# Weighted sums over key blocks 0 and 3, then 1 and 2, with the first half waiting for two causal masks

## The chip, the core and the metric

The kernel runs on one core of a Trainium2 chip. A core has a matrix engine (TensorE, PE in the profile, with its weight loads as PEld), a vector engine (VectorE, DVE), a scalar engine (ScalarE, ACT), a general engine (GpSimd, POOL) and a queue engine that only issues transfers (SyncE, SP). Each works through its own list of instructions in order; semaphores hold one back until another has got far enough. The metric is the device time of one execution in microseconds (us), lower is better.

## The reference, cut to what matters

The program computes one transformer layer on 16 sequences of 512 tokens and 128 features: a layer norm, causal attention with 16 heads of 32 features that share 4 key and value heads (rotary positions, low-rank projections), and beside it a gated feed-forward part whose operands are rounded to blocks of FP4. The part that is changed is this one:

```python
scores = jnp.einsum('bqhd,bkhd->bhqk', q, k) * scale
scores = jnp.where(causal[None, None], -jnp.inf, scores)
w = jax.nn.softmax(scores, axis=-1)
out = jnp.einsum('bhqk,bkhd->bqhd', w, v)
```

## The kernel before

**Stages.** The 16 sequences (batches) go through a software pipeline. One iteration t of the main loop does the row maxima of the scores of batch t+1, the exponentials and most weighted sums of batch t, what is left of batch t-1, and the first projections of batch t+2. It runs for t from -2 to 16; iterations 1 to 14 have all stages, and each takes some 50 us.

**Slots.** Within an iteration TensorE has 8 slots, one for each pair of heads. A slot has six tiles of scores for the row maxima (`max_tile`, L977 and L978, into three PSUM buffers that VectorE reduces in L621), between them five tiles of scores for the exponentials (`exp_tile`, L992, into two PSUM buffers that ScalarE turns into P in L815 and L818), some other jobs from the table MISC (the feed-forward matmuls L1029, transposes, projections, the output job L1076 and L1078), and at the slot's end one half of the weighted sums of a group. A tile is issued only once the buffer's reader is done with the tile two or three before it.

**Groups and the causal mask.** Four heads make a group g. P of a group holds, for each head, four key blocks of 128 keys. Key block kb is multiplied only with the queries that can see it, from kb*128 on, so the blocks 0, 1, 2 and 3 have 512, 384, 256 and 128 columns. The triangle on the diagonal of each block is set to zero by GpSimd: `causal` issues four `affine_select` (L470), one for each block and for all four heads, and each adds 1 to the semaphore `causal_done`. GpSimd does this between its other work (the products of the feed-forward part L477 to L502, the statistics of the layer norm L514 to L519, rotary positions L552 to L566), in the fixed order of its list.

**Weighted sums.** `weighted_sums` (L1011) multiplies V with P into the PSUM tile pv_ps, 32 partitions for each head: two halves for each group. The first half of group 3 of the batch before stands at the end of slot 0 and its second half at the end of slot 1; group 0 has slots 2 and 3, group 1 slots 4 and 5, group 2 slots 6 and 7. Before, the first half does the blocks 0 and 1 (896 columns a head) and the second 2 and 3 (384 columns a head), and the first half waits for all four masks of its group.

**What follows the slots.** Early in slot 1 ScalarE normalizes the next input (`normalize_x`, L885) before that slot's first exponential; it needs `shift` of GpSimd (L519), which stands behind the masks of group 3 in GpSimd's list. Those masks stand behind the addition of L480, which needs VectorE's L609 of slot 7. After that, in slot 1, VectorE reduces xn (L691) and computes scales (L596 to L600) between the maxima of L621.

Of the kernel before, what the change touches and what calls it, by code (L numbers as in the profile page):

```python
# [15 lines left out]
H, KVH = 16, 4  # L16
# [6 lines left out]
NT = S // 128  # L23
# [41 lines left out]
]  # L65

H_POWERS = [(6, 2), (6, 3), (6, 4), (7, 0)]
FIRST_T, LAST_T = -2, B


# [53 lines left out]
def build(nc, x, wqaT, wkvaT, wqb, wkvb, wout, bout, wgate, wup, wdown, cosq, sinq, cosk, sink,  # L124
          mask_q, mask_k, out):
    ctx = ExitStack()
    with ctx:
# [3 lines left out]
        def sem(name):  # L131
            return ctx.enter_context(nc.semaphore(name))
# [131 lines left out]
        causal_done = sem("causal_done")  # L264
# [179 lines left out]
        def _(pool):  # L444
# [19 lines left out]
            def causal(T, off, g):  # L464

                T.wait(pool, exp_done, NPAIR * NEXP, off, 2 * NEXP * (g + 1))
                p = P[g % 2]
                for kb in range(NT):
                    diag = p[:, :, P_COL[kb]:P_COL[kb] + 128]
                    nc.gpsimd.affine_select(out=diag, in_=diag, compare_op=ALU.is_ge, fill=0.0, base=0,  # L470
                                            pattern=[[0, GH], [1, 128]], channel_multiplier=-1).then_inc(causal_done, 1)
# [33 lines left out]
            def iteration(T):  # L505
# [4 lines left out]
                if T.has(-1):  # L510
                    causal(T, -1, 3)
# [27 lines left out]
                if T.has(0):  # L539
                    causal(T, 0, 0)  # L540
# [27 lines left out]
                if T.has(0):  # L568
                    causal(T, 0, 1)
# [231 lines left out]
        def _(act):  # L801
# [86 lines left out]
            def extra(T, slot, r):  # L888
# [23 lines left out]
                if (slot, r) == (2, 1) and T.has(2):  # L912
# [3 lines left out]
                    nc.scalar.activation(x_mag[:, :], xq[:, :], ACT.Copy, scale=2.0 ** 22).then_inc(x_powers, 1)  # L916
                if (slot, r) in H_POWERS and T.has(1):
                    f = H_POWERS.index((slot, r))
                    if f == 0:
# [21 lines left out]
        def _(pe):  # L941
# [3 lines left out]
                             start=True, stop=True).then_inc(factors_joined, 1)  # L945
# [50 lines left out]
            def weighted_sums(T, off, g, second):  # L996

                if not T.has(off):
                    return
                if not second:  # L1000
                    T.wait(pe, exp_done, NPAIR * NEXP, off, 2 * NEXP * (g + 1))
                    T.wait(pe, causal_done, NT * KVH, off, NT * (g + 1))

                    if g % 2 == 0:
                        T.wait(pe, oT_done, 2, off, g // 2)
                    if g == 0:
                        T.wait(pe, v_ready, 2, off, 2)
                for kb in ((2, 3) if second else (0, 1)):
                    width = S - kb * 128
                    for j in range(GH):  # L1010
                        last = nc.tensor.matmul(pv_ps[32 * j:32 * j + 32, kb * 128:S], V[T.par(off)][:, kb, g, :],  # L1011
                                                P[g % 2][:, j, P_COL[kb]:P_COL[kb] + width],
                                                start=(kb == 0 and g % 2 == 0), stop=(kb == NT - 1 and g % 2 == 1))
                if second:
                    last.then_inc(pv_done, 1)

# [64 lines left out]
            def iteration(T):  # L1081
                for slot in range(NPAIR):
                    max_tile(T, slot, 0)
                    exp_tile(T, slot, 0)
                    max_tile(T, slot, 1)
                    exp_tile(T, slot, 1)
                    for job in MISC[slot][0]:
                        misc_job(T, *job)
                    max_tile(T, slot, 2)
                    exp_tile(T, slot, 2)  # L1090
                    max_tile(T, slot, 3)
                    exp_tile(T, slot, 3)
                    for job in MISC[slot][1]:
                        misc_job(T, *job)
                    max_tile(T, slot, 4)
                    exp_tile(T, slot, 4)
                    max_tile(T, slot, 5)
                    for job in MISC[slot][2]:
                        misc_job(T, *job)
                    weighted_sums(T, -1 if slot < 2 else 0, (slot // 2 + 3) % 4, slot % 2 == 1)  # L1100
# [73 lines left out]
```

## Time and profile before

| | us |
|---|---|
| median of 3 runs | 894.41 (889.73 to 896.82) |
| the profiled execution | 894.42 |
| its span, first to last instruction | 892.6 |
| TensorE busy | 762.0 (85%) |
| VectorE busy | 637.8 (71%) |
| GpSimd busy | 594.1 (67%) |
| ScalarE busy | 553.3 (62%) |

Busy times are unions over the span; idle time of an engine costs something only where the chain to the end runs through it. The granted clock of TensorE is given as a share of 2.4 GHz: 1.00 is 2.4 GHz, 0.50 is 1.2 GHz. Its mean over the span is 0.973. A releaser that the profile names is inferred: for an instruction that waits for several semaphores it is the event that came last before the start.

### The profile page before, as it was taken

Reading aid. Unit: us, or ns where it says so; the run is one execution under the profiler, and the core shown is the slowest. Engines: PE = TensorE matmul, PEld = TensorE weight load, DVE = VectorE, ACT = ScalarE, POOL = GpSimd, SP = SyncE. Lnnn points to the kernel's source line nnn. Section 1 sums busy time; section 2 is a strip of 40 time slices with the busy share of each in tenths; the row PEclk is TensorE's granted clock in tenths of the full one; section 3 lists DMA queues with packets and bytes.
Section 4 is the critical chain, followed back from the end, with each engine's and each line's share of the span. In section 5 each row is a group of like instructions: output and inputs, shape, how many; then the busy total and the mean of one; then the engine's idle time right before and its main releaser. Section 6 shows DMA issues by size and latency. Waiting matters only on the chain.

```text
span 892.6 us, 18595 instructions
## 1 busy us (share of the span) xinstructions
PE 762.0 (85%) x6733; PEld 476.8 (53%) x6733; DVE 637.8 (71%) x1380; ACT 553.3 (62%) x1169; POOL 594.1 (67%) x706
## 2 busy tenths in 40 slices
PE   1367879999998989989998999989898999989785
PEld 1133545656556565656556565656556565656344
DVE  3789878777787868777787868786787868777200
ACT  1132776675766766675767666675767666675661
POOL 3435667876776768877776768777676768764631
PEclk9697999999999999999999999999999999999997
DMA  4313122322312132322312232322312232320000
GB/s 112 102 50 90 42 79 64 91 57 73 78 55 72 42 92 64 92 53 75 79 54 68 48 91 64 91 52 67 83 60 67 49 92 52 90 54 14 14 25 12
DMA packets 66262, 58.24 MB, mean 65 GB/s; under 512 B 17298, under 2 KB 56178, under 8 KB 66170
## 3 DMA queue, kind: packets, MB, share of 16 engines
q1 hardware_dynamic: 66170, 57.04, 24.1%
q8 instruction: 54, 0.88, 0.4%
q14 instruction: 38, 0.31, 0.1%
HBM read 31.81 MB, written 18.61 MB: 56 GB/s over the span
## 4 chain that ended last, share of the span: by engine, by line
PE 57%; ACT 17%; DVE 12%; issue 6%; POOL 4%; SPq 2%; DMA 1%; DVEq 0%; POOLq 0%
PE pv_ps L1011 16%; PE misc_ps L1029 8%; ACT P L815 8%; PE exp_ps L992 7%; PE max_ps L977 7%; PE misc_ps L1078 5%; DVE neg_max L621 4%; PE misc_ps L1039 3%; PE max_ps L978 3%; ACT hqT L861 2%; ACT P L818 2%; PE misc_ps L1047 2%; PE misc_ps L1076 2%; ACT up_half L854 1%; POOL P L470 1%
## 5 line engine op out<-in xcount | busy, mean ns | idle before, releaser
L621 DVE TENSOR_REDUCE neg_max<-max_ps 128x1 f32<-128x512 f32 (+3 forms) x768 | 429.3, 595 | 165.4 <-PE max_ps L978 163.3
L815 ACT ACTIVATE P<-exp_ps 128x512 f32<-128x512 f32 x512 | 291.3, 598 | 188.6 <-PE exp_ps L992 188.1
L992 PE MATMUL exp_ps<-Q,K 128*128 128x512 bf16 (+3 forms) x1024 | 244.0, 301 | 21.0 <-ACT P L815 14.4
L977 PE MATMUL max_ps<-K,Q 128*128 128x384 bf16 (+2 forms) x768 | 198.8, 278 | 18.7 <-DVE neg_max L621 16.2
L978 PE MATMUL max_ps<-Kd,Q 128*128 128x128 bf16 x1024 | 190.6, 221 | 0.9 <-DVE neg_max L621 0.8
L1011 PE MATMUL pv_ps<-P,V 128*32 128x512 f32 (+3 forms) x2048 | 168.9, 444 | 21.0 <-ACT P L818 16.5
L470 POOL TENSOR_SCALAR_AFFINE_SELECT P<-P 128x512 f32<-128x512 f32 x256 | 153.4, 634 | 20.4 <-ACT P L818 20.4
L977 PEld LDWEIGHTS max_ps<-K,Q 128*128 128x128 bf16 x768 | 76.3, 100 | 101.4 <-DVE neg_max L621 44.2
L978 PEld LDWEIGHTS max_ps<-Kd,Q 128*128 128x128 bf16 x1024 | 100.4, 99 | 35.9 <-issue 17.8
L992 PEld LDWEIGHTS exp_ps<-Q,K 128*128 128x128 bf16 x1024 | 78.3, 98 | 71.2 <-ACT P L815 45.2
L1011 PEld LDWEIGHTS pv_ps<-P,V 128*32 128x32 f32 x2048 | 62.4, 110 | 79.6 <-issue 43.8
L480 POOL TENSOR_TENSOR h<-h,h_mag 128x1408 f32<-128x1408 f32 x16 | 45.7, 2859 | 82.3 <-DVE h_mag L609 82.3
L818 ACT ACTIVATE P<-exp_ps 128x512 f32<-128x512 f32 x128 | 78.3, 612 | 28.9 <-PE exp_ps L992 28.8
L1029 PE MATMUL misc_ps<-wguT,xqT 128*128 128x352 f32 x256 | 88.7, 470 | 0.0
L477 POOL TENSOR_TENSOR h<-h,h_inv 128x1408 f32<-128x1408 f32 x16 | 41.4, 2590 | 37.2 <-DVE h_inv L600 37.2
L502 POOL TENSOR_TENSOR h<-gate_sb,up_half 128x352 f32<-128x352 f32 x64 | 59.6, 932 | 9.3 <-DVE gate_sb L634 9.2
L1029 PEld LDWEIGHTS misc_ps<-wguT,xqT 128*128 128x128 f32 x256 | 49.6, 195 | 16.1 <-issue 1.2
L1078 PE MATMUL misc_ps<-wdT,hqT 128*128 128x128 f32 (+1 forms) x384 | 55.5, 282 | 0.0
L1078 PEld LDWEIGHTS misc_ps<-wdT,hqT 128*128 128x128 f32 (+1 forms) x384 | 50.3, 199 | 0.0
L885 ACT ACTIVATE xn<-x_in,shift,rstd 128x128 f32<-128x128 f32 x64 | 26.3, 482 | 38.6 <-POOL shift L519 38.6
L483 POOL TENSOR_TENSOR h<-h,h_mag 128x1408 f32<-128x1408 f32 x16 | 45.8, 2863 | 0.0
L486 POOL TENSOR_TENSOR h<-h,h_scale 128x1408 f32<-128x1408 f32 x16 | 41.4, 2588 | 0.0
(113 smaller groups left out, 1015.8 us busy)
## 6 DMA issues: line engine op xcount, KB each, us to landing
Q<-q_scr SPq DMA_DIRECT2D x64, 224.0 KB
q_scr<-q_split SPq DMA_DIRECT2D x16, 384.0 KB, 2.6
Kd<-K SPq DMA_DIRECT2D x64, 96.0 KB
x_in<-x SPq DMA_DIRECT2D x16, 256.0 KB, 2.8
q_scr<-q_split SPq DMA_DIRECT2D x16, 256.0 KB, 2.9
x_res<-x SPq DMA_DIRECT2D x16, 256.0 KB, 5.6
out<-y SPq DMA_DIRECT2D x16, 256.0 KB, 4.8
K<-k_scr SPq DMA_DIRECT2D x64, 48.0 KB
```

Source lines behind the costliest of these rows:

```text
L470: nc.gpsimd.affine_select(out=diag, in_=diag, compare_op=ALU.is_ge, fill=0.0, base=0, pattern=[[0, GH], [1, 128]], channel_multiplier=-1). ...
L483: nc.gpsimd.tensor_tensor(t, t, mag[:, :], ALU.subtract).then_inc(quant, 1)
L502: nc.gpsimd.tensor_tensor(h[T.par(1)][:, f * F:(f + 1) * F], gate_sb[f % 2][:, :], up_half[f % 2][:, :], ALU.mult).then_inc(h_made, 1)
L621: nc.vector.tensor_reduce(neg_max[:, pr // 4, i, heads[0]:heads[0] + len(heads), pr % 4], max_ps[r % 3][:, 0:len(heads) * n].rearrange("p ...
L815: nc.scalar.activation(P[g % 2][:, hh + r % 2, col:col + 512], ps[:, :], ACT.Exp, scale=SCALE).then_inc(exp_done, 1)
L818: nc.scalar.activation(P[g % 2][:, hh:hh + 2, P_COL[2]:P_COL[2] + 256], ps[:, :].rearrange("p (h q) -> p h q", h=2), ACT.Exp, scale=SCALE) ...
L977: nc.tensor.matmul(ps[:, col:col + d], Qt, Kt[:, half, g, 0:d], start=True, stop=True)
L978: last = nc.tensor.matmul(ps[:, col + d:col + n], Qt, Kd[:, half, g, d:n], start=True, stop=True)
L992: last = nc.tensor.matmul(exp_ps[n % 2][:, col:col + width], K[par][:, half, pr // 2, kb * 128:(kb + 1) * 128], Q[par][:, pr, kb * 128:S], ...
L1011: last = nc.tensor.matmul(pv_ps[32 * j:32 * j + 32, kb * 128:S], V[T.par(off)][:, kb, g, :], P[g % 2][:, j, P_COL[kb]:P_COL[kb] + width], ...
L1029: last = nc.tensor.matmul(ps[:, 0:F], xqT[T.par(1)][:, tok[f]], wguT[:, int(job[0] == "u"), :], start=True, stop=True)
L1078: last = nc.tensor.matmul(ps[:, tok[c]], hqT[0:cn, k, tok[c]], wdT[0:cn, k, :], start=False, stop=(k == 2))
```

## The change

The order of the key blocks in the weighted sums becomes 0, 3 in the first half and 1, 2 in the second, so that both halves have 640 columns a head. GpSimd masks the blocks in that order. The first half waits until two masks of its group are done, and the second half has a wait of its own for all four. The first matmul of an accumulation is still block 0 of an even group, the last is now block 2 of an odd one.

```diff
+PV_BLOCKS = ((0, 3), (1, 2))
 ...
                 p = P[g % 2]
-                for kb in range(NT):
+                for kb in PV_BLOCKS[0] + PV_BLOCKS[1]:
                     diag = p[:, :, P_COL[kb]:P_COL[kb] + 128]
 ...
                 if not second:
                     T.wait(pe, exp_done, NPAIR * NEXP, off, 2 * NEXP * (g + 1))
-                    T.wait(pe, causal_done, NT * KVH, off, NT * (g + 1))
+                    T.wait(pe, causal_done, NT * KVH, off, NT * g + 2)
 ...
-                for kb in ((2, 3) if second else (0, 1)):
+                else:
+                    T.wait(pe, causal_done, NT * KVH, off, NT * (g + 1))
+                for kb in PV_BLOCKS[second]:
 ...
-                                                start=(kb == 0 and g % 2 == 0), stop=(kb == NT - 1 and g % 2 == 1))
+                                                start=(kb == 0 and g % 2 == 0), stop=(kb == PV_BLOCKS[1][1] and g % 2 == 1))
```

On TensorE, the end of slot 4 and the start of slot 5 before:

```order
L978 MATMUL max_ps<-Kd,Q 128x128 [waits max_read]
L978 MATMUL max_ps<-Kd,Q 128x128
L1011 MATMUL pv_ps<-P,V 32x512 [waits causal_done,exp_done]
L1011 MATMUL pv_ps<-P,V 32x512 x3
L1011 MATMUL pv_ps<-P,V 32x384 x4
L977 MATMUL max_ps<-K,Q 128x384 [waits max_read]
```

The same place in the changed kernel (its lines stand up to three lower in the file):

```order
L979 MATMUL max_ps<-Kd,Q 128x128 [waits max_read]
L979 MATMUL max_ps<-Kd,Q 128x128
L1014 MATMUL pv_ps<-P,V 32x512 [waits causal_done,exp_done]
L1014 MATMUL pv_ps<-P,V 32x512 x3
L1014 MATMUL pv_ps<-P,V 32x128 x4
L978 MATMUL max_ps<-K,Q 128x384 [waits max_read]
```

The first half keeps its place and its four matmuls of 512 columns; the four of 384 have given way to four of 128. On TensorE, the end of slot 5 before:

```order
L978 MATMUL max_ps<-Kd,Q 128x128 [waits max_read]
L978 MATMUL max_ps<-Kd,Q 128x128
L1011 MATMUL pv_ps<-P,V 32x256 x4
L1011 MATMUL pv_ps<-P,V 32x128 x4
L977 MATMUL max_ps<-K,Q 128x384 [waits max_read]
```

And in the changed kernel:

```order
L979 MATMUL max_ps<-Kd,Q 128x128 [waits max_read]
L979 MATMUL max_ps<-Kd,Q 128x128
L1014 MATMUL pv_ps<-P,V 32x384 [waits causal_done]
L1014 MATMUL pv_ps<-P,V 32x384 x3
L1014 MATMUL pv_ps<-P,V 32x256 x4
L978 MATMUL max_ps<-K,Q 128x384 [waits max_read]
```

The second half has the four matmuls of 384 columns in place of the four of 128, and its first matmul waits for masks. Nothing else on TensorE has moved, and nothing on GpSimd but the order of the four masks among themselves.

## Rows read from the trace of the kernel before

**Rows 1.** The waits over the whole span: engine, waited for, us in total, times, longest.
```profile
PE pv_ps L1011 <- ACT P L818: 16.5, 31, 0.6
PE pv_ps L1011 <- POOL P L470: 4.5, 3, 2.5
```

**Rows 2.** Timeline of slot 4: start, us, engine, line, out<-in [idle before, releaser].
```profile
411.22 0.64 ACT L818 ACTIVATE P<-exp_ps 128x512 f32<-128x512 f32 x1
...
413.08 2.39 POOL L470 TENSOR_SCALAR_AFFINE_SELECT P<-P 128x512 f32<-128x512 f32 x4
...
414.79 0.28 PE L978 MATMUL max_ps<-Kd,Q 128*128 128x128 bf16 x2
415.00 0.60 ACT L818 ACTIVATE P<-exp_ps 128x512 f32<-128x512 f32 x1
...
415.59 0.19 PEld L1011 LDWEIGHTS pv_ps<-P,V 128*32 128x32 f32 x8 [0.69 <-ACT P L818]
415.62 1.71 PE L1011 MATMUL pv_ps<-P,V 128*32 128x512 f32 x16 [0.55 <-ACT P L818]
...
417.91 1.09 ACT L815 ACTIVATE P<-exp_ps 128x512 f32<-128x512 f32 x2 [2.31 <-PE exp_ps L992]
```

**Rows 3.** Timeline of slots 2 and 3, halves without such a wait.
```profile
404.40 0.28 PE L978 MATMUL max_ps<-Kd,Q 128*128 128x128 bf16 x2
404.61 1.71 PE L1011 MATMUL pv_ps<-P,V 128*32 128x512 f32 x16
406.25 0.34 PE L977 MATMUL max_ps<-K,Q 128*128 128x384 bf16 x1
...
410.19 0.28 PE L978 MATMUL max_ps<-Kd,Q 128*128 128x128 bf16 x2
410.39 0.86 PE L1011 MATMUL pv_ps<-P,V 128*32 128x256 f32 x16
411.18 0.34 PE L977 MATMUL max_ps<-K,Q 128*128 128x384 bf16 x1
```

**Rows 4.** Timeline of GpSimd, slots 7 to 1.
```profile
384.63 2.85 POOL L480 TENSOR_TENSOR h<-h,h_mag 128x1408 f32<-128x1408 f32 x1 [5.16 <-DVE h_mag L609]
387.45 2.38 POOL L470 TENSOR_SCALAR_AFFINE_SELECT P<-P 128x512 f32<-128x512 f32 x4
...
391.68 0.20 POOL L519 TENSOR_TENSOR shift<-neg_mean,rstd 128x4 f32<-128x4 f32 x1
```

**Rows 5.** Timeline of the other engines, slots 7 to 1.
```profile
381.75 1.81 DVE L621 TENSOR_REDUCE neg_max<-max_ps 128x1 f32<-128x512 f32 x3 [1.97 <-PE max_ps L978]
...
389.98 1.71 PE L1011 MATMUL pv_ps<-P,V 128*32 128x512 f32 x16 [0.51 <-ACT P L818]
...
391.91 1.65 ACT L885 ACTIVATE xn<-x_in,shift,rstd 128x128 f32<-128x128 f32 x4 [1.92 <-POOL shift L519]
...
394.09 0.11 PEld L992 LDWEIGHTS exp_ps<-Q,K 128*128 128x128 bf16 x2 [0.30 <-ACT P L815]
```

**Rows 6.** Timeline of slot 2.
```profile
398.73 0.34 PE L977 MATMUL max_ps<-K,Q 128*128 128x384 bf16 x1 [0.42 <-DVE neg_max L621]
```

**Rows 7.** The chain that ended last, from slot 1 on and an iteration later: start, us, what.
```profile
398.08 0.61 DVE neg_max L621
...
440.34 1.69 PE pv_ps L1011 x16
```

**Rows 8.** Timeline of first halves near the end: slot 6, slots 0 and 4, the last group.
```profile
827.77 1.71 PE L1011 MATMUL pv_ps<-P,V 128*32 128x512 f32 x16 [0.44 <-ACT P L818]
...
838.07 3.04 PE L1011 MATMUL pv_ps<-P,V 128*32 128x512 f32 x16 [1.75 <-POOL P L470]
...
855.37 1.71 PE L1011 MATMUL pv_ps<-P,V 128*32 128x512 f32 x16 [0.29 <-POOL P L470]
...
874.50 4.05 PE L1011 MATMUL pv_ps<-P,V 128*32 128x512 f32 x32 [2.46 <-POOL P L470]
```

**Rows 9.** Stretches of the last batch: us, busy us of PE, PEld, DVE, ACT, POOL, PEclk, DMA share.
```profile
838.00:841.20 3.20, 3.13 (x17) 0.80 (x18) 0.00 (x0) 0.00 (x0) 3.20 (x3) 0.56 0.00 0
```

## The prediction

> **What bounds the kernel now.** I read the table of waits first, then the timeline of one whole iteration, then the end of the program. TensorE is busy 85% of the span, so an idle stretch of TensorE inside an iteration is worth having only if what follows it is not held by another engine; that has to be looked at place by place.
>
> The waits give the first half of the weighted sums 31 idle stretches of at most 0.6 us, 16.5 us in all, and three longer ones of 4.5 us together [rows 1]. The 31 are put down to ScalarE's L818. I don't believe that. In slot 4 the half starts its weight load at 415.59, and the L818 beside it ends at 415.00 + 0.60 = 415.60, after that start; and the half of group 1 needs the exponentials of slot 3 only, whose L818 ended at 411.86 [rows 2]. GpSimd's four masks end at 413.08 + 2.39 = 415.47, 0.12 before the weight load. So it is the fourth mask that releases TensorE. In slot 0 it is the same: masks to 389.83, half at 389.98 [rows 4, 5]. Of the 31, 15 are slot 4 (iterations 0 to 14), 14 are slot 0 (1 to 14), 2 are slot 6; slot 2 has none [rows 3].
>
> **The halves.** From start to what follows, the first half takes 406.25 - 404.61 = 1.64 us and the second 411.18 - 410.39 = 0.79 [rows 3], 2.43 together for 1280 columns and 16 matmuls a group. After the change each half has 640 columns and 8 matmuls, so about 1.215: the first is 0.43 shorter, the second 0.43 longer. TensorE's work is the same. The masks take the same time, only their order changes: nothing.
>
> **The second half's new wait.** The masks it waits for ended more than a slot earlier (415.47, and slot 5 had barely begun at 417.91 [rows 2]), so it is met at once. A met wait costs nothing to be seen: the half of slot 2, which has waits, starts 0.21 after the last scores, and that of slot 3, which has none, 0.20 after [rows 3]. Nothing; bounded by 0.03 us x 64 = 2 us.
>
> **Slot 4 (term 1).** Two masks are done half-way, by 413.08 + 1.2 + 0.12 = 414.4, and TensorE has its last scores of the slot at 414.79 [rows 2]. The wait goes. Its row says 0.55 idle; start to start it is 415.62 - 414.79 = 0.83 against 0.21 in slot 2, so 0.62. I take the idle row: 15 x 0.55 = 8.3, and 0.3 for the last batch [rows 8]: **8.6 us**. It lies on the path, because after it ScalarE has been idle 2.31 us for TensorE's next tile [rows 2]. The two in slot 6 give 0.45 each [rows 8], **0.9 us**.
>
> For the end of the second mask I halved the 2.39 us of the four, that is I went by starts; a mask's own row says 0.634. The Trainium skill ("Perfetto Trace Analysis", GPSIMD Engine Instruction) says that a GpSimd span is unreliable and is to be timed by the spacing of consecutive starts. By the spans two masks would take 1.27 instead of 1.2, which would take 0.07 from each of the two waits that are shortened at the end of the program and nothing from slot 4.
>
> **Slot 0.** Here too the wait of 0.51 goes, and the half is 0.43 shorter, so TensorE enters slot 1 0.9 us earlier. But it gains nothing by that itself: slot 1's exponentials stand behind ScalarE's L885, which starts at 391.91, 0.03 after GpSimd's `shift` ends at 391.88, having waited 1.92; TensorE's tile of 394.09 waits for them [rows 4, 5]. This chain goes back over the masks (all four, unchanged) to L480, which waited 5.16 for VectorE's L609, and that to VectorE's first maxima of slot 7, which waited 1.97 for TensorE [rows 4, 5]. So what slot 1 gets is what the start of slot 7 gets. What is late next in slot 0 is this chain, and I cost the wait there at nothing (bounds 0 and 0.51).
>
> **The halves as pairs (term 2).** Where both halves of a group lie on the path, 0.43 less and 0.43 more cancel: slots 2 and 3, slots 4 and 5. Group 2 is different: slot 6 is 0.43 shorter, slot 7 starts 0.43 earlier, and the chain to slot 1 leaves TensorE there, before the lengthened second half. Slot 1's own second half then has to be hidden: the second maximum tile of slot 2 waits 0.42 for VectorE, though TensorE was there [rows 6]. VectorE's work before it comes from the same chain and moves 0.43 earlier with it, so the lengthening fits into that wait. Gain 0.42 for each of iterations 1 to 14: **5.9 us**. Bounds: nothing, if the lengthened half shows, and 0.43 x 14 = 6.0.
>
> **The last batch (term 3).** There are no row maxima and no L885 any more. In slot 0 of iteration 15 TensorE waits 1.75 for the masks, and in iteration 16 2.46 [rows 8]. Each gets shorter by two masks, 1.2: **2.4 us**. The half of iteration 15 also took 3.04 instead of 1.71, with a granted clock of 0.56, almost at the 1.2 GHz level, after that idle stretch; the last group took 4.05 instead of 1.71 + 0.86 [rows 3, 8, 9]. With the wait at 0.55 the clock may stay up: 1.3 us more there and up to 1.5 at the last group. I put nothing for it in the sum and 2.8 in the range. The Trainium skill ("TensorE: Matmul & The Clock Gate", What's actually happening) says that idleness throttles the clock and activity releases it; by that rule the shorter wait of iteration 15 would keep the full clock, and the sum would be 1.3 larger.
>
> **Sum.** 8.6 + 0.9 + 5.9 + 2.4 = 17.8. The profiled execution took 894.42 (span 892.6 and 1.8 around it), the same as the median of the three runs, 894.41: 894.4 - 17.8 = **876.6 us**.
>
> **Rivals.**
> - *The second half of slot 1 is not hidden* (18%). Then term 2 is gone: 882.5. For it: the idle of 0.42 is exactly as large as what has to fit, and the chain over L596 to L600 may move less than TensorE. Against: in the chain of waits the path reaches slot 2 over a reduction of VectorE, not over the half [rows 7].
> - *The wait of slot 0 pays too* (10%). If GpSimd or ScalarE gets to L885 sooner than I think, up to 0.51 x 14 = 7.1 more: 869.5. Against: 1.92 us of ScalarE waiting for `shift`.
> - *The change does not remove what it is after* (12%). The profile names L818 of ScalarE for the 31 waits; if it is right, terms of slots 4 and 6 are gone and the half starts as late as ever: 894.4 - 5.9 - 2.4 - 0.3 = 885.8; with term 2 gone as well, 891.7. Against: a start before the end of the supposed releaser.
> - *Slower* (5%): ScalarE's exponentials set the pace after the even slots. Then the shortened first halves and the removed waits are swallowed by the next tile's wait for its buffer, while the lengthened halves of slots 1, 3, 5 and 7 delay ScalarE's next tile: 4 x 0.43 x 14 = 24 us if nothing comes back; I take half of it as won back by the queue that ScalarE then has to work off, so 894.4 + 12 = 906. It decides where ScalarE has no idle time behind a first half. Against: it idles 2.31 us there in slot 4 [rows 2].
>
> Forecast 50%; the remaining 5% is no change, from several terms failing.
>
> **How the numbers follow.** The forecast is the first case, 876.6. The range of 8 in 10 goes from 871 (the sum with the clock's 2.8 and a part of slot 0's wait) to 888 (the third rival with term 2 half gone). A measurement of this kernel can tell about 1% from no change, 8.9 us, so faster means under 885.5: the forecast, the first and second rivals, and a small part of the third give 0.79; slower, over 903.4, is most of the last rival, 0.04; 0.17 is left for no difference.
>
> **What would show it.** In slot 4 the half should start 0.21 after the last scores, with no idle. In slot 0 too, but with L885 still waiting for `shift`, and TensorE's third exponential tile of slot 1 waiting longer than 0.30. Both halves take about 1.2 us. The wait of slot 2's second maximum tile shrinks to nearly nothing. An iteration takes 440.34 - 389.98 = 50.4 us now [rows 5, 7] and should take 0.97 less, 49.4. Iteration 15's first half waits about 0.55. I am wrong if slot 4's half still starts at the end of an L818, or if TensorE's idle time reappears before an exponential tile of slot 5 or 7.

## The result, and the profile after

| | before | changed |
|---|---|---|
| median of 4 runs, us | 895.62 (889.73 to 898.62) | 868.60 (867.23 to 872.85) |
| profiled execution, us | 894.42 | 872.85 |
| its span, us | 892.6 | 871.1 |

The ratio of the means is 0.9714, 95% interval 0.9653 to 0.9776: faster, by 27.0 us from median to median. The forecast was 17.8 us and 876.6, the range 871 to 888; 868.6 lies below it. The direction and most of the places were right, the size was not.

The profile's groups of instructions: line, engine, out<-in, count | busy us, mean ns | idle before, and what ended most of it. First the changed kernel's weighted sums.

```profile
L1014 PE MATMUL pv_ps<-P,V 128*32 128x512 f32 (+3 forms) x2048 | 167.0, 440 | 1.0 <-POOL P L471 0.9 <-ACT P L816 0.2
```

The 21.0 us of TensorE waiting ahead of the weighted sums [rows 1] are down to 1.0. The timeline of the same slot 4 as [rows 2], changed kernel:

```profile
411.07 2.40 POOL L471 TENSOR_SCALAR_AFFINE_SELECT P<-P 128x512 f32<-128x512 f32 x4
...
412.70 0.28 PE L979 MATMUL max_ps<-Kd,Q 128*128 128x128 bf16 x2
...
412.91 1.28 PE L1014 MATMUL pv_ps<-P,V 128*32 128x512 f32 x16
412.91 0.60 ACT L819 ACTIVATE P<-exp_ps 128x512 f32<-128x512 f32 x1
```

The half starts 0.21 after the last scores, as slot 2's did before [rows 3], while GpSimd is still at its masks (until 413.47) and the L819 beside it has only begun. So L819 doesn't hold it here. The half takes 1.28 instead of 1.71.

Slots 7 to 1, to be held against [rows 4, 5]:

```profile
382.77 2.86 POOL L481 TENSOR_TENSOR h<-h,h_mag 128x1408 f32<-128x1408 f32 x1 [5.15 <-DVE h_mag L610]
...
385.59 2.40 POOL L471 TENSOR_SCALAR_AFFINE_SELECT P<-P 128x512 f32<-128x512 f32 x4
...
387.96 1.28 PE L1014 MATMUL pv_ps<-P,V 128*32 128x512 f32 x16
...
389.82 0.20 POOL L520 TENSOR_TENSOR shift<-neg_mean,rstd 128x4 f32<-128x4 f32 x1
...
390.06 1.65 ACT L886 ACTIVATE xn<-x_in,shift,rstd 128x128 f32<-128x128 f32 x4 [1.50 <-POOL shift L520]
...
392.24 0.11 PEld L993 LDWEIGHTS exp_ps<-Q,K 128*128 128x128 bf16 x2 [0.90 <-ACT P L816]
```

Slot 0's half waits for nothing and is 0.43 shorter, but the weight load of slot 1's third exponential tile now waits 0.90 where it waited 0.30 [rows 5], and the tile comes 4.28 after the start of the half (392.24 - 387.96) where it came 4.11 after it: L886 is still held by `shift` and starts 0.04 after its end.

To see where the time went I took the start of every half of both timelines. A stretch from one first half to a later one, in us; "forecast" is the prediction's own terms laid over the same stretches:

| stretch | before | changed | difference | forecast |
|---|---|---|---|---|
| start to group 0 of iteration 0 | 103.9 | 108.7 | +4.8 | 0 |
| to slot 0 of iteration 1 | 34.5 | 33.7 | -0.8 | -1.0 |
| iterations 1 to 13 | 654.4 | 638.4 | -16.0 | -12.6 |
| iteration 14 | 45.3 | 42.1 | -3.2 | -2.6 |
| iteration 15 | 36.4 | 33.1 | -3.3 | -1.5 |
| last group to the end | 18.1 | 15.1 | -3.0 | 0 |
| span | 892.6 | 871.1 | -21.5 | -17.7 |

The first row isn't the change's: over the 12 kernels profiled in this study, one execution each, that stretch was anywhere from 103.5 to 108.7, and none of them differs in it but by when the first masks and the first half of group 0 may go. Without it the difference is 26.3, near the 27.0 of the medians. The shortfall of the forecast is 3.4 us in iterations 1 to 13, 0.6 in iteration 14 and 4.8 in the last two stretches, where the clock is. The end of the changed kernel, to be held against [rows 8]:

```profile
822.87 1.28 PE L1014 MATMUL pv_ps<-P,V 128*32 128x512 f32 x16 [0.15 <-ACT P L816]
...
856.01 2.37 PE L1014 MATMUL pv_ps<-P,V 128*32 128x512 f32 x32 [0.86 <-POOL P L471]
```

The first half of iteration 15 took 3.04 and the last group 4.05 before; now 1.28 and 2.37, both at a granted clock of 1.00. The output matmuls behind the last group (L1076 and L1078 before) took 6.8 us, nearly all of it at 0.50, and now take 5.4 with some 3 us at half clock.

### The profile page after: what moved, and what is told of

Read it like the earlier page. It is cut to its first block, busy times and chain, and to the rows that moved or that the text cites. A ratio compares the mean times of both kernels' runs of the same rounds, so it can differ in the third digit from the quotient of the medians.

```text
span 871.1 us, 18503 instructions
## 1 busy us (share of the span) xinstructions
PE 753.0 (86%) x6641; PEld 475.7 (55%) x6733; DVE 639.6 (73%) x1380; ACT 552.8 (63%) x1169; POOL 594.3 (68%) x706
## 4 chain that ended last, share of the span: by engine, by line
PE 45%; ACT 18%; DVE 13%; POOL 13%; issue 6%; SPq 2%; another core or an unknown queue 1%; DMA 1%; POOLq 0%; DVEq 0%; ACTq 0%
PE pv_ps L1014 12%; ACT P L816 8%; DVE neg_max L622 6%; PE max_ps L978 6%; PE misc_ps L1081 5%; PE exp_ps L993 5%; POOL h L481 4%; POOL P L471 4%; PE misc_ps L1042 4%; PE misc_ps L1032 3%; PE max_ps L979 3%; ACT xn L886 2%; PE misc_ps L1050 2%; ACT hqT L862 2%; PE misc_ps L1079 2%
## 5 line engine op out<-in xcount | busy, mean ns | idle before, releaser
L993 PE MATMUL exp_ps<-Q,K 128*128 128x128 bf16 (+3 forms) x932 | 209.8, 293 | 29.3 <-ACT P L816 23.2
L1014 PE MATMUL pv_ps<-P,V 128*32 128x512 f32 (+3 forms) x2048 | 167.0, 440 | 1.0 <-POOL P L471 0.9
L979 PEld LDWEIGHTS max_ps<-Kd,Q 128*128 128x128 bf16 x1024 | 101.0, 99 | 36.7 <-issue 18.5
L1014 PEld LDWEIGHTS pv_ps<-P,V 128*32 128x32 f32 x2048 | 59.3, 109 | 71.9 <-issue 58.4
L819 ACT ACTIVATE P<-exp_ps 128x512 f32<-128x512 f32 x128 | 78.3, 612 | 28.9 <-PE exp_ps L993 28.8
L886 ACT ACTIVATE xn<-x_in,shift,rstd 128x128 f32<-128x128 f32 x64 | 26.3, 482 | 33.1 <-POOL shift L520 33.1
```

The lines of the kernel that those rows point to most:

```text
L819: nc.scalar.activation(P[g % 2][:, hh:hh + 2, P_COL[2]:P_COL[2] + 256], ps[:, :].rearrange("p (h q) -> p h q", h=2), ACT.Exp, scale=SCALE) ...
L979: last = nc.tensor.matmul(ps[:, col + d:col + n], Qt, Kd[:, half, g, d:n], start=True, stop=True)
L993: last = nc.tensor.matmul(exp_ps[n % 2][:, col:col + width], K[par][:, half, pr // 2, kb * 128:(kb + 1) * 128], Q[par][:, pr, kb * 128:S], ...
```

## The experiments

An iteration lasts 50.32 us in the kernel before and 49.11 in the changed one, measured from the start of slot 0's half, as the mean over iterations 3 to 12. It agrees to a few hundredths between kernels in the slots that an edit leaves alone: the two kernels whose edit touches none of these iterations (the last batch alone, the wait of iteration 15 alone) have 50.36 and 50.27, and nearly all of that scatter is between slots 1 and 2 (7.76 and 7.69). So it tells apart what the medians can't, but not 0.05 from nothing. Times from half to half, the same mean:

| | 0 to 1 | 1 to 2 | 2 to 3 | 3 to 4 | 4 to 5 | 5 to 6 | 6 to 7 | 7 to 0 | all |
|---|---|---|---|---|---|---|---|---|---|
| before | 6.87 | 7.74 | 5.79 | 5.23 | 8.81 | 5.52 | 5.27 | 5.11 | 50.32 |
| changed | 7.04 | 7.64 | 5.37 | 4.95 | 8.38 | 5.95 | 4.84 | 4.94 | 49.11 |
| waits alone | 7.46 | 7.58 | 5.79 | 4.61 | 8.81 | 5.52 | 5.27 | 4.52 | 49.56 |
| halves alone | 6.87 | 7.66 | 5.37 | 5.65 | 8.39 | 5.94 | 4.84 | 5.11 | 49.83 |
| group 1 waits for four | 7.03 | 7.66 | 5.36 | 5.66 | 8.38 | 5.95 | 4.84 | 4.95 | 49.83 |
| group 3 waits for four | 6.87 | 7.68 | 5.37 | 4.95 | 8.38 | 5.94 | 4.84 | 5.11 | 49.15 |
| group 2 old halves | 7.46 | 7.67 | 5.37 | 4.95 | 8.38 | 5.95 | 5.27 | 4.52 | 49.57 |
| group 3 old halves | 7.03 | 7.51 | 5.37 | 4.95 | 8.39 | 5.94 | 4.84 | 4.95 | 48.97 |
| statistics between | 6.06 | 8.25 | 5.36 | 4.95 | 8.39 | 5.95 | 4.84 | 4.95 | 48.75 |
| and scales later | 6.06 | 7.72 | 5.36 | 4.95 | 8.39 | 5.94 | 4.84 | 4.95 | 48.21 |

### The waits alone

```diff
-PV_BLOCKS = ((0, 3), (1, 2))
+PV_BLOCKS = ((0, 1), (2, 3))
```

> The halves stay as before (blocks 0 and 1, then 2 and 3; masks 0, 1, 2, 3), only the waits are the changed ones: the first half waits for two masks, the second for four. Theory (the fourth mask holds TensorE in slots 0 and 4): slot 4 gives 0.62 us in each of 15 iterations, 9.3; the two in slot 6 0.9; slot 0 nothing, since GpSimd's chain to the layer norm stays; the last batch 2.4 for the masks and some 4 more if the clock stays up: 16 to 17 us under the kernel before, and the halves of slots 0 and 4 start 0.21 after the last scores. Rival (ScalarE's L819 releases TensorE, as the profile names it): only the last batch gains, 3 to 7 us, and the halves of slots 0 and 4 start at L819's end as before.

Measured: 876.51 against 895.03, ratio 0.9786 (0.9739 to 0.9832), 18.5 us less. The timeline of slot 4:

```profile
410.44 2.39 POOL L471 TENSOR_SCALAR_AFFINE_SELECT P<-P 128x512 f32<-128x512 f32 x4
...
412.15 0.27 PE L979 MATMUL max_ps<-Kd,Q 128*128 128x128 bf16 x2
...
412.36 1.71 PE L1014 MATMUL pv_ps<-P,V 128*32 128x512 f32 x16
412.36 0.60 ACT L819 ACTIVATE P<-exp_ps 128x512 f32<-128x512 f32 x1
```

The half starts with L819, not at its end, though no edit touches ScalarE: the fourth mask was the releaser, and the profile's name for it was wrong. Slot 4 comes 0.62 sooner (5.23 to 4.61), start to start, not the 0.55 of the idle row. Slot 0's half comes 0.59 sooner and slot 1's then as much later, as expected; but slot 2 is 0.16 nearer to slot 1, which the prediction had at nothing. Over the iterations this is more than 2 us, and the 18.5 lies about that much above the 16 to 17 expected. Of the two places with the clock, one came back: the first half of iteration 15 took 1.71, the last group still 4.02.

### The halves alone

```diff
-                    T.wait(pe, causal_done, NT * KVH, off, NT * g + 2)
+                    T.wait(pe, causal_done, NT * KVH, off, NT * (g + 1))
```

> The halves and the order of the masks are the changed ones, but the first half waits for all four masks as before. Theory (equal halves pay only through the earlier start of slot 7, 0.43 to 0.54 us in each of 14 iterations): 6 to 7.5 us under the kernel before; the wait in slot 4 stays at 0.55, that in slot 0 gets no smaller. Rival (equal halves feed ScalarE and VectorE more evenly and pay by themselves in every slot): 12 us or more. Second rival (a lengthened half is exposed): no gain.

Measured: 882.81 against 895.03, ratio 0.9854 (0.9815 to 0.9894), 12.2 us less. By the time alone this is the rival's 12 or more, not the 6 to 7.5 of the theory; the trace decides. An iteration is 0.49 shorter, 6.9 us in 14, which is the theory's term, and beside it only slot 1 to 2 is shorter, by 0.08. The profiled execution is 10.9 shorter than that of the kernel before: beside iterations 1 to 13, iteration 14 is 0.9 shorter, iteration 15 0.9, and the stretch from the last group to the end 1.7, with that group at full clock (2.36). The first halves of slots 2, 4 and 6 give 0.42 or 0.43, and the second halves of slots 3 and 5 take it back; that of slot 7 doesn't, since it fits into slot 0's wait for masks, and slot 1's is hidden as well. I had expected slot 0's wait to get no smaller; no idle row is left there. Slot 4:

```profile
410.07 2.39 POOL L471 TENSOR_SCALAR_AFFINE_SELECT P<-P 128x512 f32<-128x512 f32 x4
...
411.70 0.28 PE L979 MATMUL max_ps<-Kd,Q 128*128 128x128 bf16 x2
...
412.61 1.28 PE L1014 MATMUL pv_ps<-P,V 128*32 128x512 f32 x16 [0.63 <-ACT P L819]
```

The wait in slot 4 is 0.63, not 0.55: TensorE reaches its last scores 1.63 after the masks begin, where it was 1.71 before [rows 2]. The longer second half of slot 3 gives ScalarE time to catch up: before, the weight load of slot 4's first exponential tile waits 0.19 for L818, and here nothing waits there and ScalarE is idle 0.39 for that tile.

### Group 1 or group 3 waiting for four masks again

The changed kernel, each time with one group's early wait taken back; the second one in iterations 1 to 14 only.

```diff
-                    T.wait(pe, causal_done, NT * KVH, off, NT * g + 2)
+                    T.wait(pe, causal_done, NT * KVH, off, NT * g + (2 if early(T.batch(off), g) else NT))
+    return g != 1                       # group 1
+    return g != 3 or b >= B - 2         # group 3
```

> The changed kernel, but the first half of group 1 (slot 4) waits for all four masks again. Theory (the removed wait of slot 4 is worth 0.62 us an iteration and 0.09 more that only shows with equal halves): an iteration of 49.8 us instead of 49.1, in all 10 to 11 us slower than the changed kernel, the half of slot 4 held 0.7 us more by the masks. Rival (nothing waits for masks there): no difference.

> The changed kernel, but the first half of group 3 (slot 0) waits for all four masks again, in iterations 1 to 14. The prediction costed this wait at nothing: an iteration of 49.1. New theory (an earlier slot 0 brings slot 1's maxima to VectorE sooner, and the chain of scales to slot 2 with it, 0.10 to 0.16 us): 49.2 to 49.3, in all 1.5 to 2.5 us slower. Rival (the wait is on the path in full): 49.6.

Measured for group 1: 879.05 against 893.45, ratio 0.9836 (0.979 to 0.9881), 14.4 us less than before. It is some 10 us more than the changed kernel's 868.60, as the theory had it. An iteration takes 49.83: slot 4's wait is worth 0.72. The wait's own row says 0.64, which is 0.09 more than before because TensorE arrives earlier; start to start the half is held 0.70 (415.70 - 414.79, less 0.21).

```profile
414.79 0.27 PE L989 MATMUL max_ps<-Kd,Q 128*128 128x128 bf16 x2
...
415.70 1.28 PE L1024 MATMUL pv_ps<-P,V 128*32 128x512 f32 x16 [0.64 <-ACT P L829]
```

For group 3: 868.86 against 893.45, ratio 0.9725 (0.9673 to 0.9777). An iteration takes 49.15, 0.04 more than the changed kernel, which is within the scatter. So beside equal halves slot 0's wait is worth next to nothing, as the prediction had it, and less than the 0.10 to 0.16 that I expected after the first experiments. Most of that wait had gone anyway: slot 0's half comes 0.17 sooner for the early wait (5.11 to 4.94), not 0.59 as with the old halves, since slot 7's longer half fills 0.42 of it.

### Old halves in group 2 or group 3

```diff
-                for kb in PV_BLOCKS[second]:
+                for kb in pv_blocks(T.batch(off), g)[second]:
+    return OLD if g == 2 else NEW                    # group 2
+    return OLD if g == 3 and b < B - 2 else NEW      # group 3
```

> The changed kernel, but group 2 (slots 6 and 7) has the halves 0 and 1, then 2 and 3, and its masks in that order. Theory (only this pair pays, since slot 7 starts 0.43 earlier and the chain over GpSimd leaves TensorE there): an iteration of 49.5, in all 6 us slower than the changed kernel. Rival (every pair of halves cancels, or all pay a little): 49.1 to 49.2.

> The changed kernel, but group 3 (slots 0 and 1) of batches 0 to 13 has the old halves. Theory (slot 1's longer second half is hidden behind VectorE, and slot 0's shorter first half behind GpSimd's chain): within 0.1 us of 49.1 an iteration. Rival (the longer half of slot 1 is partly exposed): faster, 48.7 to 48.9. Rival (the shorter half of slot 0 is what gives VectorE its early start): slower, 49.3 to 49.5.

Measured for group 2: 876.44 against 893.45, ratio 0.9807 (0.9751 to 0.9862), 17.0 us less than before. An iteration takes 49.57, 0.46 more than the changed kernel, and as much as with the waits alone (49.56): the whole gain of the halves comes from this one pair, because slot 7 starts sooner. The same holds in iteration 15, which takes 33.56 here and 33.14 in the changed kernel. In all it is 7.8 slower than the changed kernel, where 6 was expected. For group 3: 867.59, ratio 0.9707 (0.9649 to 0.9765), not to be told from the changed kernel by the time; an iteration takes 48.97, 0.14 less. The second maximum tile of slot 2 there:

```profile
395.19 0.34 PE L988 MATMUL max_ps<-K,Q 128*128 128x384 bf16 x1 [0.26 <-DVE neg_max L632]
```

It waits for VectorE again. It has such a wait in 10 of iterations 1 to 13, the kernel before in 11 (0.41 to 0.67), the changed one in 3 (0.20 each). So 0.14 of the longer half of slot 1 is exposed, the rest hidden. Both my theory (within 0.1) and the first rival (48.7 to 48.9) missed by a few hundredths; the truth lies between them.

### The last batch alone

```diff
+    return NEW if b == B - 1 else OLD     # blocks
+    return b == B - 1                     # early wait
```

> The change is made for the sums and masks of batch 15 alone; all other batches go as before. In the two traces the end, from slot 0 of iteration 14 on, is 9.5 us shorter after the change, 2.0 of it in iteration 14, which stays as before here. Theory (shorter waits for masks keep the clock at 2.4 GHz, and that is worth 4.3 us on top of the 2.4 for the masks): 6.5 to 8 us under the kernel before, the first half of slot 0 of iteration 15 at about 1.3 us and not 3.04. Rival (the clock at the end is chance or the same): about 3 us.

Measured: 890.65 against 895.03, ratio 0.9941 (0.9912 to 0.9971), 4.4 us less. Part of the expectation was a slip of mine: the half in slot 0 of iteration 15 belongs to batch 14, which this edit leaves alone, and it took 3.16. What the edit does reach gave 1.9 us in iteration 15, and the stretch behind the last group was 3.1 shorter. The 4.4 us fall between the theory (6.5 to 8) and the rival (about 3), and bear out the clock for the last group alone:

```profile
839.72 3.16 PE L1024 MATMUL pv_ps<-P,V 128*32 128x512 f32 x16 [1.74 <-POOL P L481]
...
874.30 2.37 PE L1024 MATMUL pv_ps<-P,V 128*32 128x512 f32 x32 [0.85 <-POOL P L481]
```

### The wait of iteration 15 alone

```diff
+    return b == B - 2 and g == 3          # early wait, old halves everywhere
```

> The kernel before; only the first half of slot 0 in iteration 15 (group 3 of batch 14) waits for two masks. Theory (TensorE's clock falls when it is idle 1.3 us or more there, and does not when it is idle 0.6): the wait goes from 1.75 to about 0.58 and the half from 3.04 to 1.71, 2.5 us in all. Rival (the low clock at this place has another cause): the wait shrinks by 1.2 and the half stays at 3.0.

Measured: 893.09 against 894.73, ratio 0.9976 (0.9953 to 1.0), no clear difference. The wait shrank as expected, the half didn't, which is what the rival said. Below the half, the end of its wait and a piece of the half itself (us, busy us of PE, PEld, DVE, ACT, POOL, granted clock):

```profile
839.98 3.07 PE L1024 MATMUL pv_ps<-P,V 128*32 128x512 f32 x16 [0.57 <-POOL P L481]
...
839.70:839.98 0.28, 0.01 (x1) 0.04 (x2) 0.00 (x0) 0.28 (x1) 0.28 (x2) 1.00 0.00 0
...
840.30:840.60 0.30, 0.30 (x4) 0.00 (x0) 0.00 (x0) 0.00 (x0) 0.30 (x2) 0.50 0.00 0
```

The clock was 1.00 through the wait and fell some 0.2 us after the half had begun. With the same wait of 0.58, the kernel with the waits alone had this half at 1.71 and a clock of 1.00. So a short wait doesn't ensure the full clock. Over the 12 profiles, iteration 15: waits up to 0.16, full clock in 6 of 6; 0.57 or 0.58, in 2 of 3; 1.33 to 1.75, in 0 of 3. At the last group: waits up to 0.86, full clock in 7 of 7, and 13.5 to 15.1 us from its start to the end; 1.28 to 2.46, in 2 of 5, and 15.1 to 18.1 us. The shorter the wait, the oftener the clock was full, but each kernel has one trace, and what decides in the cases between isn't shown. Nor do the waits account for the whole of that last stretch: with the same wait of 0.85 or 0.86 and the same 2.37 for the group, it took 13.5 where the clock was full in the output matmuls too, and 15.1 in the changed kernel, where it wasn't.

### Two steps further

The statistics of the layer norm between the masks, and then VectorE's scales behind one more maximum tile:

```diff
-                    causal(T, -1, 3)
+                    causal(T, -1, 3, PV_BLOCKS[0])
 ...                                          # var_eps, neg_mean, rstd, shift
+                if T.has(-1):
+                    causal(T, -1, 3, PV_BLOCKS[1])
```

```diff
-                reduces(1, 3)
+                reduces(1, 3, 4)
                 if T.has(2):
                     scales(...)
                 hidden_max(T, 0)
-                reduces(1, 4, 5)
+                reduces(1, 5)
```

> The changed kernel, but GpSimd does only masks 0 and 3 of group 3 ahead of the layer norm's statistics and masks 1 and 2 after them. Theory (in slot 1 TensorE waits 0.67 us for ScalarE, which waits for GpSimd's shift behind four masks): L886 starts about 0.9 us earlier and 0.6 us an iteration are won, 8 us in all, about 860. Rival (VectorE's chain of scales or TensorE itself takes over in slots 1 and 2): 0 to 3 us.

> As the kernel with the statistics between the masks, and VectorE does maximum tile 4 of slot 1 ahead of the scales of x instead of behind them. Theory (there slot 2 waits for VectorE, behind the scales): up to 0.4 us an iteration less than its 48.75, 5 us in all. Rival (the scales, and GpSimd's product of x that waits for them, are late next): no gain or a loss.

The first: 865.78 against 895.03, ratio 0.968 (0.963 to 0.973), 2.8 less than the changed kernel, where the theory said 8 and the rival 0 to 3; an iteration takes 48.75, 0.36 less. Slot 1 comes 0.98 sooner after slot 0, but slot 2 0.61 later after slot 1:

```profile
384.38 1.65 ACT L888 ACTIVATE xn<-x_in,shift,rstd 128x128 f32<-128x128 f32 x4 [0.53 <-POOL shift L520]
...
391.82 0.34 PE L980 MATMUL max_ps<-K,Q 128*128 128x384 bf16 x1 [0.61 <-DVE neg_max L624]
```

L888 waits 0.53 instead of 1.50, and VectorE, which has its scales ahead of the maximum, is late next. The second step takes that wait away: 858.25 against 894.73, ratio 0.9572 (0.9539 to 0.9605), an iteration 48.21, 0.54 less than the first step where up to 0.4 was expected. It beats both kernels; its interval lies apart from that of the change alone.

## Why the prediction came out short

- **Who releases TensorE.** Right. Waits alone and group 1 show it. That rival, the one by the profile's own label, is out. The count was off by one: in slot 4 the 31 waits are 14 (iterations 0 to 13), and slot 2 of iteration 14 has one of 0.59, where I had said it has none.
- **Halves of 1.215 us, and a met wait that costs nothing.** Right: a half gives or takes 0.42 or 0.43, and slot 5 to 6 grew by just that.
- **Slot 4 (term 1).** Right in kind, mis-sized: 0.55 taken, 0.72 found. 0.07 to 0.08 is that I took the idle row instead of start to start (0.62, which I had worked out and laid aside), the rest that TensorE reaches the wait 0.08 sooner once slot 3's half is longer. Over the 14 iterations that have this wait it is 2.4 us.
- **Slot 0 at nothing.** Right in the changed kernel, where it is worth 0.04. With the waits alone and the old halves, slot 2 followed slot 1 by 0.16 less.
- **Slot 7 (term 2).** Right: 0.42 taken, 0.46 found when it is undone. But I counted it for iterations 1 to 14 only, and iteration 15 has it too, 0.42. And since slot 7's longer half fills part of the wait behind it, the first half of iteration 15 waited 0.15 and not the 0.55 that I gave as a sign; with group 2's old halves it waited 0.57. The longer half of slot 1 is hidden but for 0.14, and the table's 1 to 2 still shrank by 0.10; that VectorE's chain starts sooner by more than I thought would do it, but isn't shown. The first rival (nothing hidden there) and the second (slot 0 pays in full) are both out; so is the slower one, by the sign of the result.
- **The last batch (term 3).** The failed step. The masks gave what I took, 1.2 at each of the two places (1.17 and 1.18). "I put nothing for it in the sum" failed: in the two traces the clock was worth 1.3 us in iteration 15 (1.71 at full clock against 3.04), and the stretch behind the last group became 3.0 shorter, 1.7 of it in the group itself (4.05 to 2.37) and 1.3 in the output matmuls, which the prediction doesn't mention. That is 4.3 of the 8.6 us by which the forecast fell short in the traces. The Trainium skill ("TensorE: Matmul & The Clock Gate", What's actually happening) says that an idle TensorE is throttled and activity releases it. That rule, which I had set beside the row, gave the right sign, and its sum of 1.3 more was nearer. But the single experiment on iteration 15 shows that the shorter wait alone doesn't bring it, so what brought the clock back at that place stays open.
- **The range.** Its low end, 871, had 2.8 for the clock and 2.8 for a part of slot 0's wait. The clock came to 4.3, slot 0 to next to nothing, and there was nothing in it for a larger term 1. 894.4 - 17.8 - 2.4 - 4.3 - 0.4 = 869.5, and 868.6 was measured.

## What to carry to other kernels

When a wait is named after an instruction that ends at or after the start it is said to release, look in the code for which semaphores stand there and compare ends. Price a wait that goes by the distance of starts against a place that has none, not by its idle row. And where one piece of work is split into two halves at fixed places, moving work between them paid here only where another engine's chain leaves between the two; that pair, not the balance, is what to look for.

## What the runs showed of the hardware

- From the end of the mask that releases it to TensorE's weight load 0.12 us passed (415.47 to 415.59) [rows 2].
- In iteration 15 the first half ran at about half clock after each of the three waits of 1.33 to 1.75 us, and after one of the three of 0.57 or 0.58. The fall didn't always come during the wait: in the kernel before it did (0.50 from 837.60 on, the half starting at 838.07), after the waits of 0.57 and 1.33 it came some 0.1 to 0.2 us into the half.
- The time to the first weighted sum, some 105 us with the loading and rounding of weights, differed by up to 5 us (103.5 to 108.7) between the 12 profiled executions, each of another kernel with the same work up to there. That is more than several of the edits here are worth.
